# Where a layer norm stands among the expert tiles: its statistics three to four tile steps later, its transposes one step later

## The reference

```
x = x + 0.5 * ffn(layernorm(x))     # 16 experts (256 -> 96 -> 256, silu gate), the best 2 per token
x = x + attn(layernorm(x))          # 16 heads, 4 key/value heads, head 128, rope, causal
x = x + 0.5 * ffn(layernorm(x))     # the same weights
```

## Time and profile before

| | |
|---|---|
| median of 3 runs | 920.71 us (913.32 to 922.92) |
| the profiled execution, its time | 920.26 us |
| its span in the profile | 918.4 us |
| TensorE busy | 790.8 us (86%) |
| VectorE busy | 658.8 us (72%) |
| ScalarE busy | 582.8 us (63%) |
| GpSimd busy | 450.0 us (49%) |
| chain that ended last, by engine | PE 60%, issue 10%, DVE 10%, POOL 8%, DMA 3% |

### The profile page before, as it was taken

How to read it: one execution, slowest core, us unless ns; L and a number is a source line. 1 busy time by engine, 2 the same in 40 slices (tenths; PEclk the granted TensorE clock), 3 DMA queues, 4 the chain that set the end, 5 groups by cost and what they waited for, 6 DMA issues and landing times.

```text
span 918.4 us, 16309 instructions
## 1 busy us (share of the span) xinstructions
PE 790.8 (86%) x4584; PEld 679.9 (74%) x4584; DVE 658.8 (72%) x1836; ACT 582.8 (63%) x1538; POOL 450.0 (49%) x410
## 2 busy tenths in 40 slices
PE   4746989879999999999999999999987978979380
PEld 3635878768788888888888888898866777868270
DVE  5813655547898888889988889978889767554163
ACT  3313756668778878877878877887765745535140
POOL 1472051476655865575665554644435840030623
PEclk9966999999999999999999999999999989999695
DMA  9355994221000100010000000000000552556454
GB/s 295 112 196 158 272 240 142 72 62 15 12 1 7 18 13 13 1 15 11 1 13 12 1 1 1 1 3 7 1 1 19 195 153 74 150 162 179 143 161 155
DMA packets 53207, 70.91 MB, mean 77 GB/s; under 512 B 7296, under 2 KB 44928, under 8 KB 52736
## 3 DMA queue, kind: packets, MB, share of 16 engines
q1 hardware_dynamic: 41024, 47.80, 17.1%
q0 software_dynamic: 9216, 16.82, 7.5%
q10 hardware_dynamic: 2880, 5.24, 2.0%
HBM read 42.80 MB, written 27.03 MB: 76 GB/s over the span
## 4 chain that ended last, share of the span: by engine, by line
PE 60%; issue 10%; DVE 10%; POOL 8%; DMA 3%; another core or an unknown queue 3%; ACT 2%; SPq 0%; DVEq 0%; POOLq 0%; ACTq 0%
PE ps L1676 50%; PE ps L1872 5%; PE ps L1730 2%; POOL sb_ropeB L1621 2%; POOL sb_xf L1624 2%; POOL sb_x L1612 1%; DVE sb_x L1472 1%; PE ps L1744 1%; PE ps L1693 1%; DVE sb_wA_raw L1266 1%; DMA xs<-sb_rowC,sb_toC 1%; POOL xs L1593 1%; POOL sb_wF L1632 1%; DVE sb_prob L1445 1%
## 5 line engine op out<-in xcount | busy, mean ns | idle before, releaser
L1676 PE MATMUL ps<-sb_wF 128*128 128x512 f32 (+2 forms) x1056 | 264.3, 378 | 9.3 <-DVE sb_wF L1462 6.8
L1676 PEld LDWEIGHTS ps<-sb_wF 128*128 128x128 f32 x1056 | 176.0, 193 | 29.1 <-issue 8.7
L1006 ACT ACTIVATE sb_prob<-sb_prob,sb_nmax 128x128 f32<-128x128 f32 (+3 forms) x256 | 142.2, 559 | 44.4 <-DVE sb_nmax L1445 41.9
L1676 PE MATMUL ps<-sb_wF,sb_wA 128*128 128x512 f32 x576 | 155.9, 406 | 7.5 <-ACT sb_ropeB L987 6.8
L1621 POOL TENSOR_TENSOR sb_ropeB<-sb_ropeB,sb_sin 128x512 f32<-128x512 f32 x80 | 111.5, 1394 | 102.2 <-ACT sb_ropeB L987 102.0
L1632 POOL TENSOR_TENSOR sb_wF<-sb_xf,sb_wF 128x384 fp32r<-128x384 f32 (+1 forms) x75 | 82.6, 1102 | 123.7 <-ACT sb_wF L999 123.5
L1472 DVE SCALAR_TENSOR_TENSOR sb_x<-ps,sb_rinv,sb_x 128x256 f32<-128x256 f32 x256 | 122.5, 478 | 23.9 <-PE ps L1676 9.1
L1676 PE MATMUL ps<-sb_wA,sb_wF 128*128 128x256 f32 x768 | 116.6, 288 | 12.8 <-DVE sb_x L1472 8.4
L1676 PE MATMUL ps<-sb_wF_raw,sb_hT 96*128 x248 | 86.1, 431 | 47.8 <-issue 23.6
L1676 PEld LDWEIGHTS ps<-sb_wF,sb_wA 128*128 128x128 f32 x576 | 102.4, 189 | 33.5 <-ACT sb_ropeB L987 14.6
L1452 DVE TENSOR_TENSOR sb_wF<-ps,sb_wF 128x512 fp32r<-128x512 f32 x160 | 109.3, 684 | 23.2 <-ACT sb_wF L1015 21.1
(11 more groups left out here) (203 smaller groups left out, 1347.5 us busy)
## 6 DMA issues: line engine op xcount, KB each, us to landing
ys<-sb_wA_raw SPq DMA_DIRECT2D x124, 128.0 KB
sb_wF_raw<-xs SPq DMA_DIRECT2D x44, 128.5 KB
sb_wA_raw<-xs SPq DMA_DIRECT2D x44, 128.5 KB
sb_work<-xs SPq DMA_DIRECT2D x36, 128.5 KB
sb_wA_raw<-in_wattn ACTq DMA_DIRECT2D x18, 256.0 KB, 3.9
sb_wF_raw<-in_wgu SPq DMA_DIRECT2D x4, 768.0 KB, 10.9
sb_wF_raw<-in_wdn SPq DMA_DIRECT2D x4, 768.0 KB, 17.5
sb_wA_raw<-in_wgu SPq DMA_DIRECT2D x4, 768.0 KB
```

Of the source, the lines that this page charges most:

```text
L1006: nc.scalar.activation(own, own, ACT.Exp, scale=-1.0, bias=nmax[:, k % 2, h:h + 1], accum_out=ssum[:, k % 2, h:h + 1]).then_inc(exp_done, 1)
L1676: return nc.tensor.matmul(out, lhsT, rhs, start=start, stop=stop)
```

## The change

It moves work between steps of the same loop. In VectorE's program the statistics of the four row tiles go from steps 12, 13, 14, 15 to 16, 16, 17, 18; mean and variance with the start of the root from 16 and 17 to 19; the refinement from 19 to 21; the normalisations from 20 and 21 to 21 and 22; the low halves from 24 to 25. TensorE's transposes go from step 22 to 23, ScalarE's high halves from 23, 24 to 24, 25. The seven projection items go from 25, 27, 29, 31, 33, 35, 37 to 26, 28, 30, 32, 34, 35, 37, and the pieces of each on ScalarE and VectorE keep their distance to it (ScalarE one and three steps behind, VectorE none and four). GpSimd's and SyncE's programs stay as they are.

```diff
+    PROJECT_AT = [26, 28, 30, 32, 34, 35, 37]
+
+    def projected_at(i):
+        return PROJECT_AT.index(i) if i in PROJECT_AT else None
...
         def first_head(i):
 
-            if i in (23, 24):
-                kk = i - 23
+            if i in (24, 25):
+                kk = i - 24
                 act.wait_ge(a0T_done, 1)
                 nc.scalar.activation(xh_at(kk), ps[:, A0BANKS[kk]], ACT.Copy).then_inc(ax_hi, 1)
-            r, odd = divmod(i - 28, 2)
-            if odd == 0 and 0 <= r <= G:
+            r = projected_at(i - 3)
+            if r is not None and r <= G:
                 rope_hi(0, -1, FIRST[r], counts=first_counts(r))
-            r, odd = divmod(i - 26, 2)
-            if odd == 0 and 0 <= r < G + 3:
+            r = projected_at(i - 1)
+            if r is not None:
                 task(0, -1, FIRST[r], counts=first_counts(r))
...
         def first_norm(i):
 
-            if 12 <= i < 12 + T:
-                dve.wait_ge(acc_in[i - 12], accumulated(1))
-                norm_stats(stats, 0, i - 12, i - 12)
-            elif i == 16:
+            for t in {16: (0, 1), 17: (2,), 18: (3,)}.get(i, ()):
+                dve.wait_ge(acc_in[t], accumulated(1))
+                norm_stats(stats, 0, t, t)
+            if i == 19:
                 mean_start(stats, mv)
-            elif i == 17:
                 rsqrt_start(mv, rs)
-            elif i == 19:
+            elif i == 21:
                 rsqrt_step(rs)
-            elif i in (20, 21):
-                for t in range(2 * (i - 20), 2 * (i - 19)):
+            if i in (21, 22):
+                for t in range(2 * (i - 21), 2 * (i - 20)):
                     ins = nc.vector.tensor_scalar(a0_row(t), x[:, 0, t], mv[:, 0, t:t + 1], rs[:, 1, t:t + 1],
                                                   ALU.subtract, ALU.mult)
                 ins.then_inc(axn_done, 1)
-            elif i == 24:
+            elif i == 25:
                 for kk in range(K):
...
-            r, odd = divmod(i - 29, 2)
-            if odd == 0 and 0 <= r <= G:
+            r = projected_at(i - 4)
+            if r is not None and r <= G:
                 rope_lo(r)
-            r, odd = divmod(i - 25, 2)
-            if odd == 0 and 0 <= r <= G:
+            r = projected_at(i)
+            if r is not None and r <= G:
                 task(0, -1, FIRST[r], counts=first_counts(r))
-            elif i == 25 + 2 * (G + 2) + 1:
+            elif projected_at(i - 1) == G + 2:
                 task(0, -1, VALUES, counts=first_counts(G + 2))
...
-            elif q.p == 1 and i == 22:
+            elif q.p == 1 and i == 23:
                 pe.wait_ge(axn_done, 2)
...
-            elif q.p == 1 and 0 <= i - 25 < 2 * (G + 3) and (i - 25) % 2 == 0:
-                if i == 25:
+            elif q.p == 1 and projected_at(i) is not None:
+                r = projected_at(i)
+                if r == 0:
                     pe.wait_ge(w_lo, LATE)
                     pe.wait_ge(ax_hi, K)
                     pe.wait_ge(ax_lo, K)
-                r = (i - 25) // 2
                 task(0, -1, FIRST[r], counts=first_counts(r))
```

## The result

The changed kernel takes 915.15 us (median of 20 runs, 909.59 to 918.85), the kernel before 920.54 (20 runs, 913.32 to 923.44). The ratio is 0.9947, with a 95% interval of 0.9931 to 0.9963: 4.9 us faster, between 3.4 and 6.4 (the two medians lie 5.4 apart). The prediction was 915.8 us. The profiled execution took 916.39 us with a span of 914.6.

What follows compares the result with a forecast made beforehand. TensorE sets the pace except where VectorE's in-order statistics wait for gathers. Stall +5.99, new place −0.9, packed norm −0.8, tail +0.3 give 4.6 us less: 915.8 us, range 910.5 to 919.8.

Steps and rivals of the forecast that it cites:

- The stall and its way to the end: VectorE's statistics wait stops TensorE, i = 14 to 17: 5.99 us with lower clock; everything later shifts by the whole sum.
- Part 1: Statistics moved from i = 12..15 to 16, 16, 17, 18: the stall goes, +5.99 us, less 0.9 at the new place.
- −0.9: At the statistics' new place, gathers for tiles 1 and 2 land late, VectorE waits: −0.9 us, between 0 and −3.7.
- half of the engines: For gathers at the new place: with one rival queue they keep about half an engine, the last landing near 133.0.
- The tile loads: Rival, slower: without the pause SyncE's loads arrive late despite 8.9 us of lead; about 922.8 us at 16 us landing; chance 0.04.
- my signs of being wrong: In the profile after: statistics DMA wait above 3 us, TensorE waiting for a tile load, or earlier last store with unchanged span.
- Part 2: Rest of the norm packed closer into VectorE's odd steps 19 and 21: net −0.8 us, from −0.4 to −1.5.
- Part 3: Transposes at 23, projections at 26 to 37: VALUES' wait for the VCOL copy goes, +0.3 us, between −0.55 and +0.66.
- The sum, 4.6 us: Whole kernel: +5.99 − 0.9 − 0.8 + 0.3 = 4.6 us gained, giving 915.7 or 916.1, stated as 915.8 us.
- A larger stall in other executions: Rival: if the typical stall at the statistics is 10 us, gain about 9 to 10, 911 us or less; chance 0.15.

Runs made afterwards that it cites:

- early4: The kernel before with the four statistics four steps earlier (i = 8 to 11), all else in place: 924.38 us.
- stats_only: The kernel before with only the norm's statistics, mean, root start and refinement moved later; normalisations, transposes and projections stay: 916.74 us.
- tail_only: The kernel before with the VCOL projection at i = 34 in place of 35, nothing else: 918.27 us, one run.
- vcol36: The changed kernel with the VCOL projection at i = 36 in place of 35: 919.90 us, one run.
- even_norm: The changed kernel with mean and start of the root at i = 18 and the refinement at i = 20: 915.45 us.
- late4_even: even_norm with four attention weight units in place of two loaded and split after the experts: 912.65 us.
- loads_after: The changed kernel with the attention weight units loaded early, up to two per step between steps 1 and 16: 914.51 us.
- loads_before: The kernel before with the 18 attention weight units loaded early, up to two per step between steps 1 and 16: 915.49 us.

## Why the prediction was right, point by point

- **The stall and its way to the end.** Right. early4, stats_only and the profile after show it: with the wait at the statistics TensorE's stop grows and goes, and the gain is kept up to the last experts. The lower clock behind the stop is not bound to it: tail_only had a stall of 4.33 us and kept the full clock. The last store landed at 182.7, where I had said 182.5.
- **Part 1: +5.99 us and −0.9 at the new place.** The sum of the two, 5.1, compares with 4.5 (first traces) and 5.7 (second) in stretch A. The −0.9 named the wrong wait. I had the gathers land late and VectorE wait for tiles 1 and 2. Nothing waited there: TensorE was already 1.5 us late, so VectorE came to the statistics at 131.51 and not at 130.0. Whether the gathers would have been late at 130.0 is tested only in part: in vcol36 VectorE came at 130.63, with the gathers issued 0.1 us later than in the kernel before, and found tile 1 landed by 131.0, where I had 131.3. My working with half of the engines was also off: 2.42 engine-us then take 4.8 us, and tile 2 lands at 132.8 and not at 133.0. That the gathers' share falls when the traffic goes on was right in kind: it was 49.1% from 128 to 132 in the profile after, between the 45.6% that I used and the 60.6% of before.
- **The tile loads.** This was my rival for a slower kernel, with 8.9 us from issue to use and about 3 us of room. The step that failed is this lead. The load that arrived late was issued at 123.52 and needed at 129.4, 5.9 us, and took 6.24 us, not the 4.5 that I had read from a drained queue. SyncE issued it late because its own program had fallen behind the evacuation that lets it load; two of its register loads on the way took 0.82 and 0.61 us, against a median of 0.27 in the kernel before. So there was no room. TensorE's weight loads waited for tiles for 0.4 and 0.9 us in the two traces of the changed kernel, 0.7 in stats_only and 1.5 in even_norm; vcol36 and late4_even show no such wait. A wait for a tile load was one of my signs of being wrong; it did not decide the sign of the change.
- **Part 2: −0.8 us.** B less its additional step is 34.42 against 33.82: −0.6. The evacuations of VectorE's steps 20 and 22 came late, as I had it. The down projections behind them, in TensorE's steps 21 and 23, had 0.17 and 0.72 us idle. even_norm gave back 0.7 us of the gross price. The second of the two waits:

```profile
142.03 0.69 PE L1681 MATMUL ps<-sb_wF_raw,sb_hT 96*128 x2 [0.72 <-DVE sb_wA_raw L1272]
```
- **Part 3: +0.3 us, between −0.55 and +0.66.** C plus one step is 12.98 against 13.60: +0.62, near the upper end; tail_only gave 0.58 by itself. The low half of the last query in step 38, which I had set against it, cost next to nothing: the gain is 0.62 of the 0.66 at most.
- **The sum, 4.6 us.** Working forward with what the traces show: 4.5 − 0.6 + 0.6 = 4.5 in the first pair, 5.7 in the second, against 4.9 by the ratio. In the first pair the price at the new place was 1.5 us and not 0.9, and the wait was another one; parts 2 and 3 came out 0.2 and 0.3 better. That the total fits to 0.1 us is luck.
- **A larger stall in other executions.** The second trace lost 7.5 us in A where the first lost 6.0. So there is some of this, but in two traces no stall of 10 us.

What stays open: why with early weight loads the changed kernel has nothing to wait for while the DMA share is still near 1, and which of the short waits before down projections in the profile after (0.37 and 0.44 us before their weight loads, with no releaser shown) come from TensorE's register loads. These took 0.47 to 0.92 us from 118 to 124 there, but 0.30 to 0.66 in loads_after, which lost nothing.

## What to carry to other kernels

A wait placed by hand in an in-order program should be placed by when its data lands in the finished schedule, and moving it later can give back more than the idle time: here the wait was 4.9 us, the loss 6.0, and 4.5 of them came back. But ask also why the data is late: here moving 4.6 MB of prefetch to a quieter time gained as much as moving the wait, because the gathers were both issued sooner and landed faster. Both together cleared stretch A, though no further gain shows in the times. When you lift a stall, the transfers that rested during it come back, so reckon the lead of every ring from the issue times in the trace and not from the number of steps in the code.

## What the hardware showed that I had not expected

The fifth gather, which adds 128 rows of 1 KB onto on-chip memory, landed 4.4 us after its issue where the other queues took 24% of the DMA engines' time meanwhile (early4), 5.5 with 56% (loads_before), and 7.0 with 70% (before). TensorE's register load, 0.30 us at rest, took up to 0.92 us from 118 to 124 in the changed kernel, with a DMA share of 1.13. The share alone does not set it: from 125.6 to 131.1, with the same share, four of them took 0.30 to 0.49 us. These are the minimum, median and longest, in ns, of the four loads from 118 to 124 us:

```profile
L1729 PEldq TENSOR_LOAD <-sb_tab x4: 472/778/920, 118.8 to 123.4; - x4
```

A wait of 2.22 us on TensorE in vcol36 was followed by the 1.2 GHz level, and stretch C grew by 3.7 us with it. A wait of 2.56 us in tail_only left the granted clock at 1.00, and in the changed kernel one of 1.68 us, before 182.98, was followed by 0.50 from 184 to 186. So in these traces the length of a wait alone does not tell whether the clock falls behind it.
